# Layer 0 of a four-layer graph network: degree matches against a PSUM iota, smaller block one-hots, a clear on ScalarE, moved table work

## The reference

```
L0: h = x @ W_t; agg = mean over the edges of a node of h[edge_col]; relu(concat(x, agg) @ W_u + b_u)
L1: x_i * (1 + eps) + sum over edges of x_j / sqrt(deg_i * deg_j)
L2: MLP((1 + eps) * x + sum over edges of x[src] * edge_weight1)
L3: MLP((1 + eps) * x + sum over edges of mish(x[src] + edge_attr @ W_e + b))
```

## Time and profile before

| | before |
|---|---|
| median of 3 runs | 8717.58 us |
| the profiled execution's own time | 8707.91 us |
| its span, first to last instruction | 8706.1 us |
| granted TensorE clock, mean | 0.837 |
| busy: TensorE, VectorE, ScalarE, GpSimd | 71%, 62%, 43%, 72% |

### The profile page before, as it was taken

The page is one execution under the profiler, slowest core; times in us unless marked ns, Lnnn a source line. Parts: engine busy times, 40 slices in busy tenths (PEclk is TensorE's granted clock), DMA queues, the critical chain, the costliest instruction groups (busy, mean ns, idle before and its releaser), DMA issues. The chain is left out here.

```text
span 8706.1 us, 153774 instructions
## 1 busy us (share of the span) xinstructions
PE 6202.1 (71%) x41943; PEld 5309.4 (61%) x41944; DVE 5376.6 (62%) x10966; ACT 3768.3 (43%) x8055; POOL 6245.2 (72%) x6523
## 2 busy tenths in 40 slices
PE   5788888888869999999634444444446777777776
PEld 2566666657769898999633333333336666666665
DVE  8898898888877888877722222222225555555554
ACT  5445355342052222222422222222236777777775
POOL 3677777777757766777477777777767777777774
PEclk7899999998789999999866666666668888888887
DMA  1122122121142222222222222222223443334432
GB/s 35 43 52 52 51 52 52 51 52 49 44 130 63 57 52 54 54 56 55 77 64 64 60 64 60 64 64 60 64 64 105 110 110 110 108 110 109 111 108 71
DMA packets 575365, 611.58 MB, mean 70 GB/s; under 512 B 114414, under 2 KB 472474, under 8 KB 574618
## 3 DMA queue, kind: packets, MB, share of 16 engines
q0 software_dynamic: 203776, 417.74, 18.9%
q1 hardware_dynamic: 294120, 145.77, 5.8%
q10 hardware_dynamic: 76722, 38.13, 1.5%
HBM read 562.68 MB, written 38.51 MB: 69 GB/s over the span
## 5 line engine op out<-in xcount | busy, mean ns | idle before, releaser
L2014 POOL DMA_INDIRECT M<-in_x,ixb x1664 | 1696.3, 1019 | 538.5 <-issue 530.0
L2195 PE MATMUL ps<-M,oh 128*128 x7056 | 1285.8, 349 | 1064.5 <-ACT M L2550 1034.1
L2061 POOL DMA_INDIRECT M<-t,ixb x1664 | 1615.7, 971 | 503.9 <-issue 498.1
L2195 PEld LDWEIGHTS ps<-M,oh 128*128 128x128 f32 x7056 | 1194.0, 253 | 1240.1 <-issue 1176.3
L2061 POOL DMA_INDIRECT M<-x,ixb x1664 | 1577.5, 948 | 503.9 <-issue 503.1
L2014 POOL DMA_INDIRECT M_any<-t,ixb x1376 | 1302.3, 946 | 501.1 <-issue 445.4
L1435 ACT ACTIVATE oht<-oneh,ot 128x128 f16<-128x128 f16 x3264 | 965.3, 387 | 979.6 <-DVE oneh L1411 979.6
L2213 DVE TENSOR_TENSOR acc<-acc,ps 128x1024 f32 x294 | 357.9, 1217 | 1587.5 <-PE ps L1776 1587.5
L1954 DVE TENSOR_TENSOR acc<-acc,ps 128x774 f32 (+1 forms) x988 | 942.7, 954 | 570.7 <-PE ps L1776 542.5
L2550 ACT ACTIVATE M<-M,wD 128x128 f32<-128x128 f32 x1664 | 517.1, 388 | 1488.2 <-DMA M<-x,ixb 1473.2
L1924 PEld LDWEIGHTS ps<-M,oh 128*128 128x128 f32 x5928 | 894.5, 209 | 266.0 <-issue 160.3
(11 more groups left out here) (306 smaller groups left out, 9256.1 us busy)
## 6 DMA issues: line engine op xcount, KB each, us to landing
er<-in_edge_attr SPq DMA_DIRECT2D x414, 256.0 KB
M<-in_x,ixb POOLq DMA_INDIRECT x1664
M<-x,ixb POOLq DMA_INDIRECT x1664
M<-t,ixb POOLq DMA_INDIRECT x1664
M_any<-t,ixb POOLq DMA_INDIRECT x1376
x<-lay SPq DMA_DIRECT2D x48, 256.0 KB, 2.4
part<-x ACTq DMA_DIRECT2D x48, 256.0 KB, 4.6
lay<-in_x SPq DMA_DIRECT2D x24, 256.0 KB, 3.9
```

What stands on the lines that cost most here:

```text
L2014: e.indirect_dma_start(M1[:, m1_slot(s, t), :] if layer else M[:, t % RING, 0:P], None, table[0:rows, :], bass.IndirectOffsetOnAxis(ap=ixb ...
L2061: e.indirect_dma_start(M2[:, t % RING, :], None, table[:, :], bass.IndirectOffsetOnAxis(ap=ixb[:, t:t + 1], axis=0)).then_inc(s_g[n % 16], 16)
L2195: ins = e.matmul(ps_flat[:, bass.ds(slot * P, P)], oh[:, j, :], tile_at(M2, tile, P), start=False, stop=False)
```

## The change

Six edits, all in the fast path:
1. The block one-hots are made 2 groups at a time, 16 instructions a supertile in place of 4, with a `yield OP` after each.
2. In the lead-in ScalarE gets 6 of 8 columns instead of 7.
3. Both degree matches read the iota from PSUM bank 6 (float32) instead of `iota8` (float16 in SBUF).
4. GpSimd's clear of `acc` becomes a ScalarE activation, ScalarE's first instruction.
5. `places` for supertile 0 runs before period 12 instead of after it.
6. `degD` is inverted directly after the last period; the 8 instructions for `lcol` run behind the 25 parts.

```diff
--- before.py
+++ after.py
@@ -1271,12 +1271,13 @@
                         cur["pay"] = tv.at()
 
                     for q in {0: (0,), 1: (1, 2), 2: (3,)}.get(i, ()):
-                        ohh_at[q] = v(lambda: e.tensor_tensor(
-                            ohh[:, 8 * q:8 * q + 8, :, :],
-                            iota4[:, :, :].rearrange("p (a b) c -> p a b c", a=1).to_broadcast([P, 8, NB, 4]),
-                            khi[:, 32 * q:32 * q + 32].rearrange("p (g a c) -> p g a c", a=1, c=4).to_broadcast([P, 8, NB, 4]),
-                            ALU.is_equal), chain=q == 0)
-                        yield OP
+                        for g in range(8 * q, 8 * q + 8, 2):
+                            ohh_at[q] = v(lambda: e.tensor_tensor(
+                                ohh[:, g:g + 2, :, :],
+                                iota4[:, :, :].rearrange("p (a b) c -> p a b c", a=1).to_broadcast([P, 2, NB, 4]),
+                                khi[:, 4 * g:4 * g + 8].rearrange("p (g a c) -> p g a c", a=1, c=4).to_broadcast([P, 2, NB, 4]),
+                                ALU.is_equal), chain=g == 0)
+                            yield OP
 
                         def count_groups():
                             for g in range(8 * q, 8 * q + 8):
@@ -1413,7 +1414,7 @@
                             def scaled_column(k, w, pf):
                                 return lambda: e.tensor_scalar(oht[:, r, k, w * P:(w + 1) * P], iota128b[:, :], tile_f[:, h, k:k + 1],
                                                                pf[:, 8 * c + k:8 * c + k + 1], ALU.is_equal, ALU.mult)
-                            shared = 7 if s < 2 else 8
+                            shared = 6 if s < 2 else 8
                             for k in range(8):
                                 if k < shared:
                                     v(one_column(k), *([lane_at[c], *free] if k == 0 else []), chain=False)
@@ -1502,7 +1503,7 @@
 
                         def match(dst_, val, width):
                             return lambda: e.tensor_tensor(
-                                dst_, iota8[:, 0:width, :],
+                                dst_, ps[:, 6, 0:width].rearrange("p (a b) -> p a b", b=1).to_broadcast([P, width, 8]),
                                 val[:, 8 * c:8 * c + 8].rearrange("p (a b) -> p a b", a=1).to_broadcast([P, width, 8]), ALU.is_equal)
                         v(match(ring_l[r], dlo, P), split, *([done[n - 6]] if n >= 6 else [tp.at()]), chain=False)
                         yield OP
@@ -2363,7 +2364,6 @@
                 stores_done(e, tal)
 
             def run_pool(e):
-                e.memset(acc_flat, 0.0).then_inc(s_z, 1)
                 tal = part_tallies()
                 for layer in range(4):
                     if layer < 2:
@@ -2404,10 +2404,21 @@
                     period(s, sort(e, "v", s + 2, tv, tp, ta))
                 e.sem_inc(s_srt, 1)
                 period(SUP - 2, degrees(e, "v", 0, HALF, tv, tp, ta))
+                tm = Tally(s_map)
+                e.wait_ge(s_v, tv.n)
+                places(e, tm, 0)
                 period(SUP - 1, degrees(e, "v", HALF, SUP, tv, tp, ta))
 
                 tp.inc()
                 v(lambda: e.tensor_copy(tot[:, :], ps[:, 7, 0:NB]), tp.at())
+                v(lambda: e.tensor_scalar(degm[:, :], degD[:, :], 0.5, None, ALU.is_gt))
+                v(lambda: e.tensor_scalar(degD[:, :], degD[:, :], 1.0, None, ALU.max))
+                v(lambda: e.reciprocal(degD[:, :], degD[:, :]))
+                e.wait_ge(s_a, 1)
+                v(lambda: e.tensor_tensor(degD[:, :], degD[:, :], degm[:, :], ALU.mult))
+                tal = part_tallies()
+                e.wait_ge(s_v, tv.n)
+                all_parts(e, "v", 0, tal)
                 v(lambda: e.tensor_tensor_scan(endp[:, :], ones_f[:, 0:NB], tot[:, :], 0.0, ALU.mult, ALU.add))
                 v(lambda: e.tensor_copy(endi[:, :], endp[:, :]))
                 v(lambda: e.tensor_scalar(endi[:, :], endi[:, :], 7, None, ALU.logical_shift_right))
@@ -2416,17 +2427,6 @@
                 v(lambda: e.tensor_tensor(endt[:, :], endt[:, :], ident[:, 0:NB], ALU.mult))
                 v(lambda: e.tensor_reduce(lcol[:, 0:1], endt[:, :], AX.X, ALU.add))
                 v(lambda: e.tensor_tensor(lcol[:, 0:1], lcol[:, 0:1], bigcol[:, :], ALU.add))
-                v(lambda: e.tensor_scalar(degm[:, :], degD[:, :], 0.5, None, ALU.is_gt))
-                v(lambda: e.tensor_scalar(degD[:, :], degD[:, :], 1.0, None, ALU.max))
-                v(lambda: e.reciprocal(degD[:, :], degD[:, :]))
-                e.wait_ge(s_a, 1)
-                v(lambda: e.tensor_tensor(degD[:, :], degD[:, :], degm[:, :], ALU.mult))
-                e.wait_ge(s_v, tv.n)
-                tm = Tally(s_map)
-                places(e, tm, 0)
-                tal = part_tallies()
-                e.wait_ge(s_v, tv.n)
-                all_parts(e, "v", 0, tal)
                 v(lambda: e.tensor_copy(ps[:, 6, 0:P], iota128[:, :]))
                 e.wait_ge(s_v, tv.n)
                 for u in range(2):
@@ -2463,7 +2463,7 @@
                 first_steps_d(e)
                 edge_dve(e, lambda m: group_dve_d(e, 3, regs, left, m, cleared), tick)
 
-            V_DEG = 12
+            V_DEG = 4
 
             def run_tensor(e, tv, tp):
                 ta = Tally(s_w)
@@ -2495,7 +2495,7 @@
                 all_parts(e, "p", 0, tal)
                 for t in tal:
                     wait(e, t[2].at())
-                tv.inc(3)
+                tv.inc(11)
                 pieces = dst_tables(e, "p", tv, tp, ta)
                 between = expand_pe(e)
                 at = [next(between)]
@@ -2527,6 +2527,7 @@
             def run_scalar(e, tv, tp):
                 ta = Tally(s_w)
                 ta.inc(W0)
+                e.activation(acc_flat, zwin[:, 0:1].to_broadcast([P, NB * W1C]), ACT.Copy).then_inc(s_z, 1)
                 e.wait_ge(s_wgt, NLD)
                 sorted_all(e, "a", tv, tp, ta, lambda s, gen: drain(gen))
                 tv.inc(V_DEG)
```

## The result

The changed kernel takes **8783.58 us** (median of 4 runs, 8779.85 to 8786.60); the kernel before, on the same chip, 8717.73 us (4 runs). The ratio is 1.0076 [1.0059, 1.0094]: slower by 0.76%, 66 us. The forecast was 8782, in a range from 8742 to 8822.

The account below looks back on a forecast made before the run. VectorE and TensorE together were taken to set layer 0's pace until GpSimd's gathers lose their lead. Terms summed to +64.6 us on the profiled 8707.9, giving 8772.5; the median's 9.7 more gave 8782, range 8742 to 8822.

Parts of the forecast that it names:

- The matches: Degree periods: 208 chunks' matches at half rate, 124 us more VectorE work, stage 454 us, +94.
- two a cycle: Degree periods: matches keep two elements a cycle, VectorE stays at 304 us, total -36, 8681 us; chance 0.08.
- The idle time: Degree periods: of VectorE's 56 us of waits, 26 stay: 18 for last counts, some 4 at each end.
- Neither rival: Degree periods: VectorE's idle time is swallowed (+68, 8744 us) or all stays (8819 us); chance 0.10 each.
- the third rival: Degree periods: TensorE gets a lower clock, counts come late, VectorE keeps all 56 us idle, 8819 us; chance 0.10.
- The clear: Lead-in: without GpSimd's memset, VectorE's sort and the gathers start earlier, -10.2 us (0 to -10.3).
- The split: Lead-in: ScalarE with 6 of 8 columns saves 3 to 4 us a supertile, -6.3 for two (0 to -18.8).
- The one-hots in the lead-in: Lead-in: sixteen smaller instructions cost VectorE 0.8 us a supertile, nothing hides it, +1.6 us.
- The one-hots in the periods: Eleven periods: smaller one-hots cost VectorE +3 us, but free GpSimd for gathers, -14 us.
- the -14: Periods 8 to 10: gathers no longer held beside large one-hots, their excess over 162 us goes (0 to -14).
- the +3 for sixteen instructions: Eleven periods: VectorE's 19 idle us a period hide most of the smaller one-hots' cost, +3 us (0 to +9).
- Places and table work: End of layer 0: first part starts earlier, -6.5 us (-4 to -8); `places` before period 12 costs +3 (0 to 5.8).

Follow-up runs that it names:

- e2: The kernel before with only the matches' iota operand changed to float32 in PSUM: 8802.52 us, ratio 1.0102.
- e3: The changed kernel with the matches' iota read as float16 from SBUF, one value repeated by step 0: 8786.44 us, one execution.
- e9: e1 with the matches' float16 iota, each value stored eight times (step 1), read from PSUM: 8672.72 us, ratio 0.9948 to the kernel before.
- e1: The changed kernel with the matches reading the float16 iota in SBUF again: 8679.14 us, ratio 0.9959 to the kernel before.
- e5: e1 with the clear of `acc` back on GpSimd: 8692.38 us, one execution.
- e7: e1 with the block one-hots in four large instructions a supertile again instead of sixteen small: 8699.12 us, one execution.
- e10: e1 with the block one-hots in eight instructions of four groups a supertile instead of sixteen: 8665.00 us, one execution.
- e8: e1 with `places` behind the last period again, in front of the 25 parts: 8682.71 us, one execution.

## Why the prediction was right

**The matches.** Predicted 1216 and 286 ns, measured 1213 and 277. That makes 121.6 us more in the two periods, where the sum has 124. VectorE's work 428 us, measured 430.3, of which some 5 are `places`, which the sum has in another term. Idle 26, measured 25.3; stage 454, measured 454.5 to 455.6. +94 for the matches and +3 for `places` in the stage, measured +94.9 for both, where the two terms make 97. Edit 3 alone (e2, without `places` there) made the stage 92.2 us longer. The half rate was put down to the float32 operand in PSUM, since L1936 shares it. That was incomplete: L1936 has a repeated value too, and the runs show that the repeat alone does it (e3) and PSUM alone does not (e9). Without the row of L1936 the rival "two a cycle" would have been reasonable, and e9 shows that a form of this edit exists for which it is true.

**The idle time.** Neither rival came: VectorE's idle time shrank from 56 to 25 us; it neither vanished nor stayed. The total of 26 was right partly by luck, since two misses cancel: the wait before L1523 was 9.1 us where I took 18, and the waits before the matches themselves, 7.0 us here and 7.6 before, are not in my sum. The clock did fall, to 0.69, as the third rival said, but TensorE's matmuls grew only to 388 ns each from 343, in the kernel before and in e1, and VectorE waits for its steps less than before (8.0 us at the adds, where it was 33.6).

**The clear** -10.2: e5 gives -10.7 to -10.8. ScalarE's clear took 10.74 us, under the bound of 13.4.

**The split** -6.3: about -2 at the first add. **The one-hots in the lead-in** +1.6: nothing to be seen (e7, 0.1 us). With the clear the lead-in comes to -12.7, where the terms make -14.9.

**The one-hots in the periods.** The eleven periods went from 1788.3 to 1780.8, -7.5 where the terms make -11. All of them now last 161.4 to 162.5 us. Periods 8 to 10 got shorter by 1.3, 6.3 and 4.9 us, together 12.5, near the -14. The others got longer by up to 0.9, together 5.0. So the term that was mis-sized most is the +3 for sixteen instructions: VectorE's idle time hides less of them than I took, and e10 gets 6 to 10 us back with eight.

**Places and table work** -6.5 and +3: the way from the last add to layer 1's first add measured -6.5, of which e8 gives 3.4 to `places`. The +3 lies inside the stage. In e1 it is nothing (e8); where VectorE bounds, the kernel after has 454.5 us and e2, without `places` there, 451.8, which fits a cost of 3 but is no more than like executions differ by.

The sum: 64.6 predicted, 68.1 measured at layer 1's first add, and 65.9 between the medians. By stretch, predicted and measured: lead-in -14.9 and -12.7, periods 0 to 10 -11 and -7.5, degree periods +97 and +94.9, the way into layer 1 -6.5 and -6.5. The misses of +2.2, +3.5 and -2.1 cancel in part, which is luck. The forecast stood on the one large term, whose row was there. The median of 8782 rests on one step more, 9.7 us from the profiled execution to the median. It was the profiled execution of the kernel before that was quick; that of the kernel after took 8784.63 where its like was put at 8772.5, and 9 of these 12 us are layer 3.

## What to carry to other kernels

Price an edit on the engine that will be the bound after it, not on the one it relieves: here VectorE went from 84 to 94% busy so that the gathers got quicker, and with the other edits in place nothing waited for the gathers there (e1). The 16-bit comparison of two tensors kept its double rate with an innermost step of 1 and lost it with a step of 0. Where a value is to be repeated, store it repeated. One operand in PSUM makes GpSimd's gathers beside such instructions quicker (945 ns in place of 1113); that this gave time here is not shown. Cutting a long VectorE instruction with two SBUF operands into pieces frees GpSimd, and a few pieces do: half as many here did as much for GpSimd and saved VectorE 7 us of work.

## What the runs showed of the hardware that was not expected

- A float16 operand in PSUM at step 1 does not cost VectorE its double rate (682 ns, beside 683 from SBUF).
- A step of 0 on the innermost dimension of one operand costs the whole double rate, 1215 ns, with all data float16 in SBUF.
- The same gather takes 945 ns beside matches with an operand in PSUM, whatever their length (682 or 1213 ns), 1113 ns beside SBUF matches of 683 ns, and 1470 beside SBUF matches of 1215 ns.
- A step of 0 on a dimension further out costs nothing: the values of the match have one in e1 and e9, 683 and 682 ns.
- ScalarE writes 12642 float32 elements a partition in 10.74 us, about as long as GpSimd's memset takes (10.63), and VectorE goes on beside it (L1257: 0.23 us).
- Two of the chips took 11168 and 11244 us for the kernel before, which takes 8704 to 8718 us on the others.
